# Rotary embedding in a two-layer transformer kernel: the exchanged half from a VectorE shuffle instead of a second product

## What is computed

```python
def _rope(x):                       # x: batch, token, 16 heads, 8
    x1, x2 = (x[..., :half], x[..., half:])            # half = 4
    return jnp.concatenate([x1 * cos - x2 * sin, x1 * sin + x2 * cos], axis=-1)
...
xn = _adaln(x, noise_emb, n1_w[i], n1_b[i])
q, k, v = jnp.split(xn @ qkv_w[i].T, 3, axis=-1)
x = x + _attn(_rope(q), _rope(k), v, src_mask) @ so_w[i].T
xn = _adaln(x, noise_emb, n2_w[i], n2_b[i])
q, k, v = _rope(xn @ cq_w[i].T), _rope(context @ ck_w[i].T), context @ cv_w[i].T
x = x + _attn(q, k, v, ctx_mask) @ co_w[i].T
xn = _adaln(x, noise_emb, n3_w[i], n3_b[i])
x = x + gelu(xn @ f1_w[i].T + f1_b[i]) @ f2_w[i].T + f2_b[i]
```

## Time and profile before

| | |
|---|---|
| median of 3 runs | 2422.79 us (2421.81 to 2427.86) |
| profiled execution, span from first to last instruction | 2430.0 us |
| TensorE matmul busy | 2038.2 us, 84% |
| VectorE busy | 1686.1 us, 69% |
| ScalarE busy | 1538.0 us, 63% |
| GpSimd busy | 882.0 us, 36% |
| mean granted TensorE clock | 0.917 |
| the chain that ended last | TensorE 56%, VectorE 14%, issue 4%, ScalarE 4% |

### The profile page before, as it was taken

One profiled execution on the slowest core, in us unless ns is written; L12 is line 12 of the kernel. 1 busy time (PEld: TensorE's weight loads), 2 busy tenths in 40 slices (PEclk: granted clock), 3 DMA queues, 4 the chain that ended last, 5 costly groups with the idle time before them and its releaser, 6 DMA issues.

```text
span 2430.0 us, 38348 instructions
## 1 busy us (share of the span) xinstructions
PE 2038.2 (84%) x14066; PEld 897.6 (37%) x14066; DVE 1686.1 (69%) x3124; ACT 1538.0 (63%) x1937; POOL 882.0 (36%) x1362
## 2 busy tenths in 40 slices
PE   3662999926789999999999999999999999988651
PEld 2331666611223333333343333333433333333321
DVE  7667121236678888888878887888778888886456
ACT  2441323203567788888777877888788887768442
POOL 2542202012334444443444434444444444333331
PEclk9776999956999999999999999999999999989665
DMA  1000000032332334333333344332253334321100
GB/s 49 1 1 2 34 12 24 0 82 53 64 64 68 70 89 97 85 70 80 80 80 75 80 90 78 86 85 62 60 108 88 79 71 92 86 52 36 32 6 9
DMA packets 148642, 144.40 MB, mean 59 GB/s; under 512 B 30887, under 2 KB 136163, under 8 KB 148451
## 3 DMA queue, kind: packets, MB, share of 16 engines
q1 hardware_dynamic: 148463, 142.05, 26.3%
HBM read 79.01 MB, written 60.51 MB: 57 GB/s over the span
## 4 chain that ended last, share of the span: by engine, by line
PE 56%; DVE 14%; issue 4%; ACT 4%; POOL 1%; DMA 1%; SPq 0%; POOLq 0%; DVEq 0%; ACTq 0%
PE ps L1268 14%; PE ps L1232 7%; PE ps L1221 6%; DVE smax L1766 6%; PE ps L1346 6%; PE ps L1387 4%; PE ps L1378 4%; PE ps L1280 4%; ACT big L1501 2%; DVE rot L1782 2%; PE ps L1321 2%; PE ps L1305 2%; PE ps L1243 1%; PE ps L1255 1%; PE ps L1338 1%
## 5 line engine op out<-in xcount | busy, mean ns | idle before, releaser
L1501 ACT ACTIVATE big<-ps 128x1024 f32<-128x1024 f32 x960 | 955.6, 1026 | 264.6 <-PE ps L1232 246.0
L1766 DVE TENSOR_REDUCE smax<-ps 128x2 f32<-128x1024 f32 x768 | 921.7, 1221 | 271.7 <-PE ps L1221 265.9
L1268 PE MATMUL ps<-big,vaug 128*32 128x512 f32 x3072 | 414.1, 618 | 3.2 <-ACT big L1501 3.1
L1221 PE MATMUL ps<-k,q 49*128 49x512 bf16 x1536 | 294.9, 392 | 68.5 <-DVE smax L1766 34.5
L1232 PE MATMUL ps<-q,k 52*128 52x512 bf16 x1536 | 296.7, 389 | 11.9 <-DVE smax L1766 5.3
L1697 POOL CAST mparts<-smax 128x16 bf16<-128x16 f32 x96 | 19.4, 202 | 574.5 <-DVE smax L1766 574.5
L1221 PEld LDWEIGHTS ps<-k,q 49*128 49x128 bf16 x1536 | 72.9, 94 | 318.2 <-DVE smax L1766 106.3
L697 DVE SCALAR_TENSOR_TENSOR state<-ps,share,state 128x128 f32<-128x128 f32 x128 | 36.0, 344 | 196.0 <-PE ps L668 196.0
L1346 PE MATMUL ps<-xnT,w 128*128 128x512 f32 x288 | 167.5, 668 | 0.9 <-ACT xnT L1538 0.9
L685 ACT ACTIVATE big<-ps 128x512 f32<-128x512 f32 x128 | 76.5, 598 | 144.7 <-PE ps L659 144.7
L1773 DVE TENSOR_REDUCE maxima<-ps 128x8 f32<-128x616 f32 x192 | 144.6, 794 | 31.5 <-PE ps L1255 30.0
(11 more groups left out here) (290 smaller groups left out, 2982.2 us busy)
## 6 DMA issues: line engine op xcount, KB each, us to landing
q<-scratch_queries SPq DMA_DIRECT2D x48, 384.0 KB, 6.1
k<-scratch_keys SPq DMA_DIRECT2D x48, 384.0 KB
cq<-scratch_cross_queries SPq DMA_DIRECT2D x48, 384.0 KB, 5.9
scratch_queries<-rparts SPq DMA_DIRECT2D x24, 384.0 KB, 2.4
scratch_keys<-rparts SPq DMA_DIRECT2D x24, 384.0 KB, 2.6
scratch_cross_queries<-rparts SPq DMA_DIRECT2D x24, 384.0 KB, 2.5
scratch_queries<-rparts SPq DMA_DIRECT2D x24, 256.0 KB, 2.7
scratch_keys<-rparts SPq DMA_DIRECT2D x24, 256.0 KB, 3.2
```

Source lines behind the costliest of these rows:

```text
L1221: last = nc.tensor.matmul(out[:, u], m.q6[rows, v % 2, 2 * g + pr, qt * P:(qt + 1) * P], m.k6[rows, v % 2, 2 * g + pr, :], start=True, sto ...
L1268: last = nc.tensor.matmul(m.ps[32 * j:32 * j + 32, pv_bank, :], of_head(m.vaug, v % 2 * TB + kt, g, j), of_quad("self", q)[:, j, :], start ...
L1501: nc.scalar.activation(of_quad(kind, p // 2)[:, p % 2 * 2:p % 2 * 2 + 2, :], banks("exp" if kind == "self" else "cross exp", p), ACT.Exp, ...
L1766: nc.vector.tensor_reduce(m.smax[:, n % 2, qt, :, pr], banks("max", i), AX.X, ALU.max).then_inc(s_read["self"], 1)
```

## The change

The weights `qr`, `kr`, `cqr` and `ckr` go, with their columns in the weight arrays and their share of the weight loads. Each product is done once. VectorE then issues two instructions of 128 x 512 in place of one of 128 x 1024: a `stream_shuffle` that writes the product with lane i taken from lane i xor 4 within each 32 partitions, and the multiplication by the cosine. The multiplication of the shuffled half by the sine is a new GpSimd instruction ahead of the addition in `rotate`, and the addition waits for it through a semaphore. For the context keys one product of 308 columns takes the place of four of 154, with the same split of the work.

```diff
+OTHER_HALF = [lane ^ (HD // 2) for lane in range(32)]
...
-    "PE product cross 0": (10290,),
-    "PE product cross 1": (10446,),
+    "PE product cross": (10290,),
     "DVE rope cross": (10566,),
...
-    "PE product query 0": (-7307,),
-    "PE product query 1": (-7150,),
+    "PE product query": (-7150,),
...
-    "PE product key 0": (-7024,),
-    "PE product key 1": (-6822,),
+    "PE product key": (-6822,),
...
-    "PE product context 0": 6383,
-    "DVE rope context 0": 6468,
-    "PE product context 1": 7733,
-    "DVE rope context 1": 7818,
+    "PE product context": 7733,
+    "DVE rope context": 7818,
...
-                got = nc.tensor.matmul(banks(kind, i)[:, half, :], w_of(m, names[half]), m.xnT[:, xn[of_turn, i], :], start=True, stop=True)
-                if half:
-                    got.then_inc(x_ps[kind], 1)
+                nc.tensor.matmul(out[:, 0, :], w_of(m, name), m.xnT[:, xn[of_turn, i], :], start=True, stop=True).then_inc(x_ps[kind], 1)
...
             def rotate(kind, i):
-                pool.wait_ge(x_read[kind], 2 * (i + 1) if kind == "context" else i + 1)
+                pool.wait_ge(x_read[kind], i + 1)
                 x = turned(kind, i)
...
+                else:
+                    r_chain.link(nc.gpsimd.tensor_tensor(x[:, 1, :], x[:, 1, :], m.cs[:, 1, :], ALU.mult))
                 nc.gpsimd.tensor_tensor(x[:, 0, :], x[:, 0, :], x[:, 1, :], ALU.add).then_inc(x_rot[kind], 1)
...
-                nc.vector.tensor_tensor(m.rot[:, rot[kind, i]], banks(kind, i), m.cs[:], ALU.mult).then_inc(x_read[kind], 1)
+                out, product = m.rot[:, rot[kind, i]], banks(kind, i)[:, 0, :]
+                nc.vector.stream_shuffle(out[:, 1, :], product, OTHER_HALF)
+                nc.vector.tensor_tensor(out[:, 0, :], product, m.cs[:, 0, :], ALU.mult).then_inc(x_read[kind], 1)
...
+                product = m.ps[:, aux, 0:NC_ALL]
+                nc.vector.stream_shuffle(m.rot_c[:, 1, :], product, OTHER_HALF)
+                nc.vector.tensor_tensor(m.rot_c[:, 0, :].rearrange("p (b n) -> p b n", n=N_CTX), product.rearrange("p (b n) -> p b n", n=N_CTX),
+                                        m.cs[:, 0:1, 0:N_CTX].to_broadcast([P, B, N_CTX]), ALU.mult).then_inc(x_read["context"], 1)
```

66 lines of the change are left out of this document (28 added, 38 removed).

## The result

| | before | after |
|---|---|---|
| median of 4 runs each, same chip | 2423.35 us (2421.81 to 2427.86) | 2457.72 us (2455.76 to 2460.92) |
| profiled execution, span | 2430.0 us | 2455.0 us |

The ratio is 1.0139, with a 95% interval of 1.0125 to 1.0154: slower, by 34 us. The two profiled executions differ by 25 us only, since that of the kernel before is 7 us above its median. The forecast was 2428 us in a range of 2404 to 2448, so the time lies outside the range, on the side to which 0.33 was given.

What follows compares the result with a forecast made beforehand. TensorE bounds a visit by the sum, but ScalarE is also full behind queries and keys. +6 us for the cross queries and -1 for the ends gave +5 on the profiled span, 2428 us on the median, range 2404 to 2448.

Steps and rivals of the forecast that it cites:

- What goes, what comes: Prices: TensorE loses 76 us of products; VectorE's pair costs 0.07 us more; GpSimd gains 1.35 us per rotation, 97 in all.
- Place one: Query and key products and ropes: a gain of 0.4 us a visit, bounds 0 to 0.5.
- rival C: Slower: shuffle or GpSimd's part of the rope chain dearer than thought, delaying ScalarE's first part; 2437 us, chance 0.22.
- Place two: Cross queries: late GpSimd rotation delays the first feed-forward product; net loss 0.3 us a visit, 22 visits, +6 us.
- The context keys: Context product: only an estimated 0.6 us of TensorE a layer saved; no wait of ScalarE for their rotation was forecast.
- The ends: First rotation, last but one cross attention, last cross product and first visits: together -1 us, between -8 and +4.
- Rival D: Slower: TensorE idling at queries and keys lowers its clock; one fall in four visits costs 30 us, 2458; chance 0.11.

Runs made afterwards that it cites:

- no_sine: Changed kernel without GpSimd's multiplication by the sine table in all four rotations, shuffle kept; ratio 0.9930 to the kernel before.
- two_sine_query: Changed kernel with context product, rope and rotation early, bias behind the cross-query rotation, and the queries' sine multiplication on VectorE; ratio 0.9986 to the kernel before.
- prod_first: Changed kernel with the one product of queries and of keys at the place of the first of the former two; ratio 1.0207 to the kernel before.
- cross_two: Changed kernel with the cross queries from two products again; ratio 1.0124 to the kernel before.
- bias_late: Changed kernel with GpSimd's addition of the feed-forward bias moved behind the rotation of the cross queries; ratio 1.0087 to the kernel before.
- filler: Changed kernel plus an unread 256-column matmul per visit between the transpose of the cross maxima and the unit transpose; ratio 1.0140 to the kernel before.
- ctx_early: Changed kernel with the context keys' product, shuffle, cosine and GpSimd rotation moved ahead; ratio 1.0088 to the kernel before.
- qk_two: Changed kernel with queries and keys from two products each again; ratio 1.0065 to the kernel before.
- ctx_two: Changed kernel with the context keys from two products again; ratio 1.0149 to the kernel before.
- two_rope_first: Changed kernel with context rotation early, bias behind the cross-query rotation, and the queries' product and rope earlier, the rope ahead of the row maximum; ratio 1.0002 to the kernel before.

## Why the prediction was wrong

By its own steps:

- **What goes, what comes: right, but for TensorE's total.** The group of the products fell from 167.5 to 84.6 us of busy time (76 were worked out). TensorE's busy time as a whole fell by 58 us only, where about 80 was to show; other groups of matmuls grew, for instance that of the values from 414.1 to 419.9. The shuffle takes 727 ns (forecast 690, bounds 600 to 1220), with the step of 0.62 us to the next instruction. The cosine takes 674, GpSimd's multiplication 1271 (forecast 1268), and the step from it to the addition is 1.34 to 1.35 us, as forecast. The page "VectorE: DVE Perf Modes" of the Trainium skill (The perf-mode tier table) has 2400 against 2293 ns for 2048 elements. My estimate of 0.1 us for 512 had not been scaled; a quarter of the difference is an estimate of 0.03. The trace shows 0.04 (727 against 688).
- **Place one: the mechanism right, the size wrong.** TensorE's side came as written (0.44 of 0.5 us, each wait at its place). ScalarE's was off: the first part was to come 0.22 us later than before and came 0.39 later, since VectorE waits 0.16 us in front of its shuffle, which starts only at 1699.76, where TensorE's product, itself held by a buffer for 0.55 us, ends. This buffer was in no step. The copy behind it then comes 0.12 us later instead of 0.03 earlier. The term was 0.4, inside bounds of 0 to 0.5, and measured 0.11. I had taken it near its upper bound. no_sine and two_sine_query show that 0.2 to 0.36 us are there once GpSimd's multiplication is out of the way; prod_first shows that the chain through it moves the visit one for one, which is rival C's mechanism.
- **Place two: right, and it inherits that error.** The prediction took 0.66 us of delay less 0.4 from place one, 0.26. With 0.11 in place of 0.4 the same step gives 0.55; measured are 0.62 to 0.65. Over 24 visits the term was +6 and is +15. cross_two and bias_late show the place: 0.73 and 0.78 us come back.
- **The context keys: a term that was missing.** This is the step that failed most. The forecast counted 0.6 us of TensorE a layer among what goes and had nothing on GpSimd's queue there. The walk along GpSimd's queue that was made at place two would have found it here: three multiplications (1.27, 1.27, 0.8 us) were moved ahead of the context's first part, in ScalarE's written order, with exponentials behind it. The price is 2.8 us a layer beyond the 0.62 of every visit, some 17 us, half of the loss: by filler 1.8 of the 2.8 are the wait (11 us) and 1.0 the fall of the clock behind it (6 us). ctx_early gives it back by order alone, and qk_two shows that the first two of the three decide.
- **The ends:** -1 was forecast, about 0 comes out in the two profiled executions (1.0 us later at 760 us, 1.8 lost in the first visit of the last layer, 3.1 won behind it).
- **Rival D, the clock: partly.** The steady visits did show a clock below 1.00, which the prediction named as its sign of error. As a sign it was a poor one: the clock of the kernel before was not 1.00 throughout either, as the prediction had read, but fell once, to 0.57 in the window from 1504 to 1508 us of a third visit. 17.1 against 1.7 us are lost in the profiled executions. A fall that lost 1.7 us made an ordinary visit of after 1.1 us longer, and one that lost 3.4 us 2.9, against the 5 or 6 us of the prediction. And I had tied the falls to place one, where most of them follow the context's wait: in after, ctx_two, cross_two and bias_late one stands behind it in 17 of 20 third visits, in filler and prod_first in 6 of 10; with queries and keys undone nothing is lost, with the context moved 3.4 us. At place one a fall is the exception in after (one of seven); two_rope_first has three there. Two third visits, of ctx_early and of ctx_two, there:

```profile
1201.73:1205.73 4.00, 2.50 (x17) 1.00 (x12) 3.22 (x5) 2.20 (x4) 1.54 (x5) 1.00 0.01 3
1205.73:1209.73 4.00, 3.99 (x25) 1.33 (x24) 3.83 (x7) 2.83 (x4) 3.19 (x3) 1.00 0.05 14
```

```profile
1200.06:1204.06 4.00, 2.49 (x18) 1.12 (x12) 3.22 (x5) 2.21 (x4) 1.54 (x5) 0.96 0.01 3
1204.06:1208.06 4.00, 4.00 (x16) 1.34 (x14) 2.66 (x6) 1.86 (x3) 3.19 (x3) 0.61 0.04 12
```

TensorE was busy for 2.5 of 4 us both times; once the clock stays and once it falls, mostly to 1.2 GHz. What decides between the two stays open.

The sum by the measured terms: 24 x 0.62 = 15 for places one and two together, 6 x 2.8 = 17 for the context keys, 32 of the 34 us. Of these, some 6 are the clock's share by filler, rival D's kind of loss in another place. The causes of rival C did not come: the shuffle and GpSimd's two cost what was forecast, and its 2437 us is 20 short.

## What to carry to other kernels

In an order written out by hand, an operation that moves to a less busy engine can be paid for by whoever stands next in line on the engine that waits for it: go through every place where it is issued, the rare ones too, and ask what is queued ahead of its result. If a gain and a loss of one step pass through the same saturated engine, price the gain at its lower bound and carry it into the later steps in that form. Before undoing such a change, move the one independent instruction that stands ahead of the late result: the bias alone was worth 0.8 us a visit, and the context's product, shuffle and rotation 3 us a layer.

## What was not expected of the hardware

- The shuffle comes with a second record in the trace, LOAD_MASK_SELECT, of 0.01 us. The shuffle of 128 x 512 fp32 from PSUM takes 727 ns where a multiplication of that size takes 674, and 505 against 460 at 128 x 308.
- With TensorE busy alike, the clock falls in some executions and visits and not in others: 2.50 and 2.49 of 4 us in the two windows above, and the third visits of filler, with the same wait of 2.73 us and a fall in three of five. Two kernels whose ordinary visits are equal to 0.01 us lost 0.1 and 13.8 us.
